# Attention 1 of a two-layer gated block: from scores by token rows to turned scores, with the row maxima as two more rows of the operand

## The reference

```python
q = q.reshape(b, HD, H, -1)          # HD = 16, H = 16, last axis 1024 queries
k = k.reshape(b, HD, H, -1)          # last axis 64 keys
v = v.reshape(b, HD, H, -1)
scores = jnp.einsum('bdhn,bdhk->bhnk', q, k) / HD ** 0.5
prob = jax.nn.softmax(scores, axis=-1)
x = jnp.einsum('bhnk,bdhk->bdhn', prob, v)
return _conv1x1(x.reshape(b, HD * H, -1), Wm, bm)
```

## Time and profile before

| | |
|---|---|
| median of 3 runs | 1495.08 us (1495.05 to 1495.64) |
| the profiled execution's own time | 1496.8 us |
| its span (first to last instruction) | 1495.1 us |
| TensorE busy | 1377.2 us, 92% |
| VectorE busy | 971.4 us, 65% |
| ScalarE busy | 745.9 us, 50% |
| GpSimd busy | 426.3 us, 29% |
| mean granted TensorE clock | 0.966 |

### The profile page before, as it was taken

The page is one execution under the profiler, slowest core; times in us unless marked ns, Lnnn a source line. Parts: engine busy times, 40 slices in busy tenths (PEclk is TensorE's granted clock), DMA queues, the critical chain, the costliest instruction groups (busy, mean ns, idle before and its releaser), DMA issues. The chain is left out here.

```text
span 1495.1 us, 28528 instructions
## 1 busy us (share of the span) xinstructions
PE 1377.2 (92%) x10782; PEld 1120.8 (75%) x10782; DVE 971.4 (65%) x1564; ACT 745.9 (50%) x1881; POOL 426.3 (29%) x473
## 2 busy tenths in 40 slices
PE   6998789989989999987999999999779999999388
PEld 6998778979889898865888888888556666666144
DVE  4363277777767767565232256578567999998597
ACT  4231167766757767763111110113157777777396
POOL 0010001101010110010110232232358888887324
PEclk9999889999999999999999999999889999999789
DMA  6742454553544536464445452112332222221023
GB/s 224 244 155 85 90 126 117 139 146 77 145 110 120 147 96 167 125 197 150 166 167 197 157 210 99 56 36 84 113 81 65 62 64 64 63 64 43 1 85 141
DMA packets 127910, 174.93 MB, mean 117 GB/s; under 512 B 27799, under 2 KB 96919, under 8 KB 127792
## 3 DMA queue, kind: packets, MB, share of 16 engines
q1 hardware_dynamic: 127792, 173.26, 39.9%
HBM read 86.94 MB, written 35.29 MB: 82 GB/s over the span
## 5 line engine op out<-in xcount | busy, mean ns | idle before, releaser
L1148 ACT ACTIVATE a_prob<-a_psS,a_negmax 128x256 f32<-128x256 f32 x512 | 236.7, 483 | 158.6 <-DVE a_negmax L1063 158.4
L1063 DVE TENSOR_REDUCE a_negmax<-a_psS 128x4 f32<-128x1024 f32 x128 | 154.1, 1204 | 68.1 <-PE a_psS L956 66.5
L881 POOL COPY a_recip<-a_recip_head 128x256 f32<-128x256 f32 x64 | 25.6, 400 | 526.5 <-DVE a_recip_head L1113 526.5
L931 PE MATMUL a_psQ<-a_xT_hi,wide 128*128 128x256 f32 x912 | 170.9, 288 | 0.4
L1375 PE MATMUL m_psY<-wide,m_a_hi 128*128 128x512 f32 x512 | 159.3, 393 | 6.8 <-DVE m_a_lo L1423 6.8
L1375 PE MATMUL m_psY<-w_ffn,m_a_hi 128*128 128x512 f32 x512 | 158.3, 390 | 0.0
L966 PE MATMUL a_psT<-ident,a_prob 128*128 128x128 f32 x1024 | 138.0, 279 | 14.1 <-issue 6.1
L931 PEld LDWEIGHTS a_psQ<-a_xT_hi,wide 128*128 128x128 f32 x912 | 138.7, 189 | 9.1 <-issue 5.9
L1165 ACT COPY a_probT<-a_psT 128x512 f32<-128x512 f32 x208 | 115.8, 609 | 36.7 <-PE a_psT L966 35.6
L966 PEld LDWEIGHTS a_psT<-ident,a_prob 128*128 128x128 f32 x1024 | 116.7, 143 | 23.0 <-issue 12.7
L931 PE MATMUL a_psQ<-a_xT_lo,wide 128*128 128x256 f32 x456 | 127.5, 280 | 0.0
(11 more groups left out here) (233 smaller groups left out, 3013.9 us busy)
## 6 DMA issues: line engine op xcount, KB each, us to landing
a_q_stack<-a_q_hi SPq DMA_DIRECT2D x128, 128.0 KB, 2.6
a_q_stack<-a_q_lo SPq DMA_DIRECT2D x128, 128.0 KB, 2.6
c_raw<-lay_ctxT SPq DMA_DIRECT2D x16, 512.0 KB, 4.8
rows<-in_x SPq DMA_DIRECT2D x8, 1024.0 KB, 6.4
scratch_o<-a_oT SPq DMA_DIRECT2D x16, 512.0 KB, 3.0
m_x<-in_x SPq DMA_DIRECT2D x8, 1024.0 KB, 5.9
scratch_x<-m_x SPq DMA_DIRECT2D x8, 1024.0 KB, 5.1
b_q_stack<-b_q_hi SPq DMA_DIRECT2D x64, 128.0 KB, 2.3
```

What stands on the lines that cost most here:

```text
L881: nc.gpsimd.tensor_copy(recip[:, t % 2], recip_head[:, t % 2].unsqueeze(3).broadcast_to([P, TT, JH0, HD0])).then_inc(recip_ready, 1)
L931: last = nc.tensor.matmul(bank[:, 0:S], w[:, kt, t * P:(t + 1) * P], a[:, kt, :], start=(kt == 0 and w is wq.hi and a is xT_hi), stop=(kt ...
L1063: nc.vector.tensor_reduce(negmax[:, n % 2, :], psS[:, bank:bank + 2, :].rearrange("p a (j k) -> p (a j) k", k=S), AX_X, ALU.max, negate=Tr ...
L1148: last = nc.scalar.activation(prob[:, n % 2, j, :], psS[:, 2 * (n % 2) + j // 2, (j % 2) * S:(j % 2 + 1) * S], ACT.Exp, bias=negmax[:, n % ...
```

## The change

`attn1_stage` is written anew. A batch is now four steps `k`; a step belongs to a tile of 512 queries (half `h`) by 8 heads (half `t`).

- `scores` multiplies only the query's high part (`q_hi`) by the keys, 128 queries at a time and 512 columns, into a single bank `psS`. DVE takes negated maxima (`negmax`, L1984). The next product waits for that maximum (`max_ready`), since there is one bank. These scores serve for nothing else.
- `turn_shift` transposes the 16 negated maxima of 512 queries to 16 rows (L1854), ACT copies them (`copy_shift`, L2101), and SP writes them as two rows under the stacked query by four transfers of one destination partition (`stack_shift`, L1749).
- `turned_scores` multiplies a pair of heads: stationary is `kT` (98 rows: keys high, high, low, and two rows of ones; 2x64 columns), moving is `q_stack` (98 rows: query high, low, high, and the two rows of maxima; 512 queries). The result is the shifted scores, keys by rows, so ACT's exponential (L2108) writes what `values` needs. The transposes, the copies `probT`, the subtraction on DVE and the additions on POOL fall away.
- `values` runs on four column groups with 512 columns, and 8 further products with a 0/1 operand (`sum_of`, L1888) give the sums of the probabilities on 32 rows of each group. DVE takes their reciprocals, 256 columns at once (L2001), twice a batch; they are split in high (ACT, L2112) and low (POOL) and spread over the rows by 8 products (`spread_reciprocals`, L1901, L1902) before `normalise_o` (L2009) multiplies.
- Keys for `kT` come as six transfers of 32 partitions (L1721); ACT makes the high parts (`high_keys`, L2081), DVE the low ones (`low_keys`, L1991).
- The rows of query weight, key weight and biases are interleaved on the host (`woven`), so that 32 neighbouring partitions by 4 take one transfer of 256 KB for four head pairs: three transfers per tile (L1738).
- Tables and both weights come laid out from the host. The fp8 weight is loaded at the start of `ffn1_stage`. All loops are unrolled.

The core of the diff:

```diff
+    def tile_of(k):
+        return k % CT1, k // CT1
+    def output_of(b, k):
+        return (b, 0, 0) if k == 3 else (b - 1, *((1, 0), (0, 1), (1, 1))[k])
...
+        def scored_tile(b, k):
+            return (b + 1, k - 1) if k else (b, TILES - 1)
...
+            def stack_query(a, k):
+                t, h = tile_of(k)
+                if a:
+                    sp.wait_ge(psP_full, 4 * TILES * (a - 1) + PJ * (k + 1))
+                sp.wait_ge(q_lo_ready, TILES * a + k + 1)
                 cols = slice(h * HALF_N, (h + 1) * HALF_N)
...
+                for part, src in enumerate((q_hi, q_lo, q_hi)):
+                    sp.dma_start(plain(q_stack)[part * 2 * HD1:(part + 1) * 2 * HD1, t * PJ:(t + 1) * PJ, cols],
+                                 plain(src)[:, k % 2, :]).then_inc(q_stacked[k], 16)
...
+            def stack_shift(a, h):
+                if a:
+                    sp.wait_ge(psP_full, 4 * TILES * (a - 1) + 2 * PJ * (h + 1))
+                sp.wait_ge(shift_ready, 2 * a + h + 1)
+                for t in range(CT1):
+                    for e in range(2):
+                        lo = t * HT1 + e * PJ
+                        sp.dma_start(plain(q_stack)[STACKED + e:STACKED + e + 1, t * PJ:(t + 1) * PJ, h * HALF_N:(h + 1) * HALF_N],
+                                     plain(shift)[lo:lo + PJ, h, :]).then_inc(shift_stacked[h], 16)
...
-            def transposes(b, n):
-                pe.wait_ge(exp_done, NT * b + n + 1)
-                for t in range(CT1):
-                    pe.wait_ge(psT_copied[t], NT * b + n + 1)
-                    for j in range(4):
-                        last = nc.tensor.transpose(psT[:, t, j * P:(j + 1) * P],
-                                                   prob[:, n % 2, (4 * t + j) * P:(4 * t + j + 1) * P], ident[:, :])
-                    last.then_inc(psT_full[t], 1)
...
+            def scores(a, k, i):
+                t, h = tile_of(k)
+                n = 4 * (TILES * a + k) + i
+                if i == 0:
+                    pe.wait_ge(q_ready, TILES * a + k + 1)
+                    if k < CT1:
+                        pe.wait_ge(kbd_ready, CT1 * a + t + 1)
+                if n:
+                    pe.wait_ge(max_ready, n)
+                nc.tensor.matmul(psS[:, :], q_hi[:, k % 2, i * P:(i + 1) * P], kbd[:, a % 2, t, :, :].rearrange("p h k -> p (h k)"),
+                                 start=True, stop=True).then_inc(scores_full, 1)
+            def turn_shift(a, h):
+                pe.wait_ge(max_ready, 4 * (TILES * a + 2 * h + 2))
+                turns = 4 * a if h == 0 else 4 * a + 2
+                if turns - 2 > 0:
+                    pe.wait_ge(o_ready, turns - 2)
+                for i in range(4):
+                    last = nc.tensor.transpose(psB[0:NH1, i * P:(i + 1) * P], negmax[:, h, i, :], ident[:, :])
+                last.then_inc(shift_full, 1)
+            def turned_scores(b, k, j):
+                t, h = tile_of(k)
+                n = PJ * (TILES * b + k) + j
+                if j == 0:
+                    pe.wait_ge(q_stacked[k], QDMAS * (b + 1))
+                    pe.wait_ge(shift_stacked[h], 64 * (b + 1))
+                    if k == 0:
+                        pe.wait_ge(kT_ready, b + 1)
+                if n >= 2:
+                    pe.wait_ge(exp_done, n - 1)
+                nc.tensor.matmul(psP[:, n % 2, :], kT[0:ROWS, b % 2, t * PJ + j, :, :].rearrange("p e k -> p (e k)"),
+                                 q_stack[0:ROWS, t * PJ + j, h * HALF_N:(h + 1) * HALF_N], start=True, stop=True
+                                 ).then_inc(psP_full, 1)
...
+            def values(b, k):
+                t, h = tile_of(k)
+                n = TILES * b + k
+                if k == 0:
+                    pe.wait_ge(v1_loaded[b % 2], 16 * (b // 2 + 1))
+                pe.wait_ge(exp_done, PJ * (n + 1))
+                if n:
+                    pe.wait_ge(o_copied, n)
+                for j in range(PJ):
+                    last = nc.tensor.matmul(psO[j * 2 * HD1:(j + 1) * 2 * HD1, :], v1[:, b % 2, t * PJ + j, :], probT[:, j, :],
+                                            start=True, stop=True)
                 last.then_inc(psO_full, 1)
...
+                for part in range(2):
+                    for j in range(PJ):
+                        last = nc.tensor.matmul(psM[j * 2 * HD1:(j + 1) * 2 * HD1, 0:S], sum_of[:, part, t, :],
+                                                probT[:, j, part * S:(part + 1) * S],
+                                                start=(t == 0 and part == 0), stop=(t == CT1 - 1 and part == 1))
+                last.then_inc(sums_full, 1)
...
+            def spread_reciprocals(b, h, t):
+                n = 2 * b + h
+                if t == 0:
+                    pe.wait_ge(recip_low, n + 1)
+                    pe.wait_ge(shift_ready, min(n + 2, 2 * B))
+                else:
+                    pe.wait_ge(o_ready, 2 * n + 1)
+                for part in range(2):
+                    nc.tensor.matmul(psB[:, part * S:(part + 1) * S], spread[:, t, part, :], recip_hi[:, :], start=True, stop=False)
+                    last = nc.tensor.matmul(psB[:, part * S:(part + 1) * S], spread[:, t, part, :], recip_lo[:, :],
+                                            start=False, stop=True)
+                last.then_inc(psB_full, 1)
...
+            for b, k in STEPS:
+                if scored:
+                    scores(sa, sk, 0)
+                if turned:
+                    turned_scores(b, k, 0)
+                if k == 1 and real(b):
+                    turn_shift(b, 1)
+                if k == 3 and real(b + 1):
+                    turn_shift(b + 1, 0)
+                if asked:
+                    query(b + 1, k, 0)
+                if scored and k % 2:
+                    scores(sa, sk, 1)
+                if turned:
+                    turned_scores(b, k, 1)
+                if asked:
+                    query(b + 1, k, 1)
+                if scored:
+                    scores(sa, sk, 2 if k % 2 else 1)
+                if turned:
+                    turned_scores(b, k, 2)
+                if put:
+                    output(outputs, ob, t, h, 0)
+                if scored:
+                    scores(sa, sk, 3 if k % 2 else 2)
+                if turned:
+                    turned_scores(b, k, 3)
+                if put:
+                    output(outputs, ob, t, h, 1)
+                    outputs += 1
+                if scored and k % 2 == 0:
+                    scores(sa, sk, 3)
+                if spreads:
+                    spread_reciprocals(sb_, sh_, 0)
+                if turned:
+                    values(b, k)
+                if spreads:
+                    spread_reciprocals(sb_, sh_, 1)
...
-            def shift(b, n):
-                dve.wait_ge(max_ready, NT * b + n + 1)
-                nc.vector.tensor_tensor(prob[:, n % 2, :].rearrange("p (h k) -> p h k", h=NH1),
-                                        psS[:, n % 2, :].rearrange("p (h k) -> p h k", h=NH1),
-                                        maxes[:, n % 2, :].unsqueeze(2).broadcast_to([P, NH1, NK1]),
-                                        ALU.subtract).then_inc(shifted, 1)
...
+            def low_keys(b):
+                dve.wait_ge(kT_high, b + 1)
+                lo, hi = 2 * 2 * HD1, STACKED
+                for e in range(2):
+                    last = nc.vector.scalar_tensor_tensor(kT[lo:hi, b % 2, :, e, :], krep[lo:hi, :, :], row_mask[lo:hi, e:e + 1],
+                                                          plain(kT)[lo:hi, b % 2, :, e, :], op0=ALU.mult, op1=ALU.subtract)
+                last.then_inc(kT_ready, 1)
+            def reciprocals(b, h):
+                n = 2 * b + h
+                dve.wait_ge(sums_full, 2 * n + 2)
+                if n:
+                    dve.wait_ge(psB_full, 2 * n)
+                    dve.wait_ge(recip_low, n)
+                nc.vector.reciprocal(recip[:, :], psM[:, 0:S]).then_inc(recip_ready, 1)
+            def normalise_o(b, h, t):
+                n = 4 * b + 2 * h + t
+                dve.wait_ge(psB_full, n + 1)
+                dve.wait_ge(o_copied, n + 1)
+                if b:
+                    dve.wait_ge(out_full, 4 * (b - 1) + 2 * h + 2)
+                nc.vector.tensor_tensor(o[:, t, h * HALF_N:(h + 1) * HALF_N], psB[:, :], o_raw[:, t, :], ALU.mult
...
+            for b, k in STEPS:
+                sa, sk = scored_tile(b, k)
+                sb_, sh_ = (b - 1, 1) if k == 0 else (b, 0)
+                scored, spreads = real(sa), k % 2 == 0 and real(sb_)
+                if b == -1 and k == 0:
+                    normalise_x2(0, 1)
+                if scored:
+                    maximum(sa, sk, 0)
+                if spreads:
+                    reciprocals(sb_, sh_)
+                if scored:
+                    maximum(sa, sk, 1)
+                if scored:
+                    maximum(sa, sk, 2)
```

(47 more changed lines are left out.)

677 lines of the change are left out of this document (256 added, 421 removed).

## The result

The changed kernel takes 1531.28 us (median of 4 runs, 1530.32 to 1534.23) against 1495.07 (4 runs) before: ratio 1.0245 [1.0228, 1.0263], slower. I had forecast 1505, with 1524 as the upper end. The sign was right and the loss 36 us instead of 10.

What follows compares the result with a forecast made beforehand. PE and DVE, both full, were taken to bound the kernel. The profiled 1496.8 us plus 5.4 for the stage and 5 for the clock gave 1507.2, and 1505 as the runs' median; range 1486 to 1524.

Steps and rivals of the forecast that it cites:

- A full batch, 40.3: Loop of the attention stage: PE's need of 31.8 us plus waits of 2.8, 2.75, 1.4, 0.9 and 0.7, against 37.6 before.
- TensorE's need: PE's own work per batch: 31.8 us (31.1 to 33.5), 7.6 each odd step and 8.3 each even one.
- The losses: PE's waits per batch: step 1 2.8 us, step 2 2.75, reciprocal 1.4 in step 2 and 0.9 in step 0, step 3 0.7.
- The clock, +5: Half clock after PE's new pauses: a fall in every second of batches 1 to 6, +5 us (0 to +20).
- The edges, 143.7: Stage outside five full batches: 28 us before batch 0, batches 0, 1, 7 at 32.2, 36, 26, tail 21.5; before 151.8.
- The four steps behind it: Steps b=-1 before batch 0, running at the pace of copy, maximum and half clock; 28 us until batch 0 turns.
- my second rival: Rows of maxima land late for the turned scores: step 3 loses 1.4 us seven times, batch 7 2.6; 1517, chance 0.12.
- My 203 GB/s for busy engines: Transfer rate of a busy microsecond, used for the tables at the stage's start: about 0.9 MB in 4.5 us.
- "Cost nothing" for the weight: Early fp8 weight load, 9.0 us to land, needed 14.7 after the last stage's start: hidden by the fp8 scale's chain.
- The sign: Direction of the whole kernel's time: slower 0.58, faster 0.30, same 0.12.
- the rival "faster": Reciprocal at 0.41 us and values at 1.72 give batches of 38.2 and no clock falls: 1487, chance 0.30.
- my slope: DVE's reciprocal of 256 elements, priced from two rows at 7.6 ns per element: 2.05 us.

Runs made afterwards that it cites:

- filled_right: Changed kernel with unused products, sized at 0.86 us each, in TensorE's pauses before batch 0 and in batches 0 and 2 to 6: 1516.7 us, 1.0148.
- early_start: Changed kernel with TensorE's wait for the tables moved to the first products using them, ScalarE's table copy in the second step: 1526.0 us, 1.0220.
- shift_first: Changed kernel with the four transfers of the rows of maxima issued ahead of the three stacking the query, in step 3: 1551.8 us, 1.0391.
- orders_and_start: Changed kernel with reordered VectorE side work and high_keys, later fp8 weight, later table wait, rows of maxima ahead of query stackings: 1511.6 us, 1.0110.

## Why the prediction was wrong

Of the 26 us between 1505 and 1531, about 11 are the clock (16 where I had 5), about 11 the edges without it, and 3 the last stage; full batches at full clock add under 1.

- **A full batch, 40.3:** near at full clock, 40.5 in filled_right, but by luck. TensorE's need was larger, near 34 (40.5 less the waits below) where I had 31.8: step 3 takes 8.6 with a wait of 0.4, so 8.2 where I had 7.6, since a score product with its turned one takes 0.58 to 0.60 there, not 2 x 0.23. Values and sums take 1.86 (I had 1.9); a set of four products of 512 columns takes 0.88, what one plain product does (0.86), so the column groups run side by side. The losses were smaller: 2.1 in step 1 (2.8), 2.6 and about 0.9 in step 2 (2.75 and 1.4), 0.4 in step 3 (0.7), none for the reciprocal in step 0 (0.9). The two errors cancel.
- **The clock, +5: the step that failed first.** I assumed "a fall in every second of batches 1 to 6". It fell in each of batches 2 to 6, seven times in all where I had three, and in batch 0, where I had none. Its cost is 10.7 + 5.4 = 16 by filled_right's windows, and 14.6 by the medians. A fall cost 1.5 on average in batches 2 to 6 (I had 1.7), so the size was right and the count wrong. I had the pauses somewhat too long (2.07 and 2.60, not 2.8 and 2.75), and priced what follows from them at a third. Shown: with the pauses filled, or gone, the falls went. Not shown: why a pause lowers the clock in one batch and not in the next.
- **The edges, 143.7: the second.** The windows at the edges are 159.9, or 154.5 without batch 0's half clock. The wait for the tables before the first product was in my sum and about right (6.2 us, 6.8 measured). The four steps behind it, for which I had counted the pace of copy and maximum at half clock only, took 28.3 and not 21.8. The stackings of 256 KB take 6.8 us to land here, where those of 128 KB took 2.4, and the rows of maxima stand behind them: the wait for `b_shift`, 2.75 in the start, was my second rival, in the one place where I had not put it. In batches 1 to 7 it did not happen. My 203 GB/s for busy engines did not hold either: from 1095 to 1104 us the DMA share was 0.95 at 123 GB/s. For batch 0, 33.5 at full clock against 32.2, I had left out the waits behind `low_keys` and the reciprocal. Orders took 3.2 off the start by the wait for the tables (early_start), 1.9 by that for the rows (shift_first), and 6.1 by both (orders_and_start). What is over in the four steps beside the wait for the rows is not split further. Nor are the 2.1 of batch 7 and the tail.
- **"Cost nothing" for the weight:** wrong by 2.9; putting the transfer behind the all-reduce took 2.4 of the median. I had looked for who needs the weight and not for who uses the same way at that moment. That GpSimd fetches something ahead of its all-reduce is inferred; that the transfer delays it is shown.
- **The sign:** the rival "faster" needed a batch under 39; it was 41.0 to 43.7, and 40.5 even at full clock.

On the reciprocal, 128x256 measured 1.75 us; both my slope (2.05; from the two rows it is 2.08) and the estimate by the Trainium skill that I gave (near 2) were above it, and the copy's 0.41 far below.

## What to carry to other kernels

Look at where each engine's side work stands in its queue before changing the work itself: the same instructions took 1531 us in one order and 1492 in another. Price a pause of TensorE together with the half clock that may follow, and where pauses come twice a batch, count a fall in most: six or seven of ten here. When a wait or a transfer is moved ahead, list what stands behind it on that queue, and when a transfer is "hidden", who else moves data in that time.
